# Input loaded in three parts, and the activations between two convolutions laid out with four patches interleaved, in a fused vision-tower kernel

## The reference

```
x = (x - mean) / (1e-06 + std) / sqrt(16)            # per patch and colour
x = conv2d(x, conv1_w, conv1_b); residual = x        # 3 -> 64 channels, 3x3
x = gelu(group_norm(x, gn1_g, gn1_b))                # 32 groups
x = conv2d(x, rconv1_w, rconv1_b)                    # 64 -> 64, 3x3
x = gelu(group_norm(x, gn2_g, gn2_b))
x = residual + conv2d(x, rconv2_w, rconv2_b)         # 64 -> 64, 3x3
x = conv2d(x, proj_w, proj_b, stride=16, pad=0)      # patch -> 192 numbers
```

## Time and profile before

| | |
|---|---|
| median of 3 runs | 1460.72 us (1459.5 to 1462.84) |
| profiled execution | 1465.48 us, of which the span is 1463.7 us |
| PE busy | 1365.6 us (93%) |
| DVE busy | 1081.5 us (74%) |
| ACT busy | 864.3 us (59%) |
| POOL busy | 576.4 us (39%) |
| granted TensorE clock, mean | 0.984 |

### The profile page before, as it was taken

One profiled execution on the slowest core, in us unless ns is written; L12 is line 12 of the kernel. 1 busy time (PEld: TensorE's weight loads), 2 busy tenths in 40 slices (PEclk: granted clock), 3 DMA queues, 4 the chain that ended last, 5 costly groups with the idle time before them and its releaser, 6 DMA issues.

```text
span 1463.7 us, 38493 instructions
## 1 busy us (share of the span) xinstructions
PE 1365.6 (93%) x14042; PEld 1022.2 (70%) x14042; DVE 1081.5 (74%) x4148; ACT 864.3 (59%) x2127; POOL 576.4 (39%) x1116
## 2 busy tenths in 40 slices
PE   4999988888999999999999999999999978998889
PEld 2865653344888688858976897788688867754647
DVE  3864358898888988888888889888988854544520
ACT  1434446777667777777767767767777630344451
POOL 1100035555544544544554554544545521162600
PEclk9999999999999999999999999999999988998999
DMA  7799945545554455455545554555455589300000
GB/s 218 208 268 275 266 118 162 183 127 132 139 151 134 128 150 143 131 140 143 147 125 142 150 149 119 147 152 138 128 154 136 149 226 255 79 1 1 1 1 17
DMA packets 125178, 206.17 MB, mean 141 GB/s; under 512 B 20028, under 2 KB 88188, under 8 KB 124478
## 3 DMA queue, kind: packets, MB, share of 16 engines
q1 hardware_dynamic: 124990, 203.71, 51.0%
HBM read 103.11 MB, written 20.70 MB: 85 GB/s over the span
## 4 chain that ended last, share of the span: by engine, by line
PE 63%; DMA 9%; issue 7%; DVE 7%; POOL 6%; SPq 6%; ACT 2%; POOLq 0%; ACTq 0%; DVEq 0%
PE rc L637 26%; PE pj_st L728 8%; DMA sb_acts<-sb_hst 7%; PE rc L638 6%; PE pj_st L732 4%; POOL sb_tmp L487 4%; PE rc L658 3%; PE rc L657 3%; DMA sb_wall_arena<-scratch_fold 2%; SPq L372 2%; SPq L311 2%; PE c L693 2%; DVE sb_bn L952 1%; PE rc L1440 1%; PE rc L1528 1%
## 5 line engine op out<-in xcount | busy, mean ns | idle before, releaser
L637 PE MATMUL rc<-sb_acts,sb_rwd 128*64 128x512 f16 x1764 | 559.3, 390 | 17.4 <-DMA sb_acts<-sb_hst 17.4
L638 PE MATMUL rc<-sb_acts,sb_rwd 128*64 128x512 f16 x1764 | 560.3, 390 | 0.0
L487 POOL TENSOR_TENSOR sb_tmp<-sb_mst,sb_half_neg 128x8 f32<-128x8 f32 x200 | 350.7, 1754 | 456.3 <-DVE sb_mst L973 453.4
L554 ACT ACTIVATE sb_f32q<-c,sb_gsh,sb_gsc 128x128 f32<-128x128 f32 x792 | 298.7, 458 | 273.7 <-POOL sb_gsh L497 273.7
L637 PE MATMUL rc<-sb_acts,sb_rwl 128*64 128x512 f16 x1176 | 361.8, 389 | 0.0
L638 PE MATMUL rc<-sb_acts,sb_rwl 128*64 128x512 f16 x1176 | 361.1, 389 | 0.0
L728 PE MATMUL pj_st<-sb_wall_arena 128*64 128x384 f16 x1792 | 308.6, 334 | 6.9 <-DVE sb_wall_arena L992 6.6
L576 ACT ACTIVATE sb_g2f<-rc,sb_gsh,sb_gsc 128x128 f32<-128x128 f32 x784 | 298.1, 481 | 4.5 <-POOL sb_gsh L497 4.5
L732 PEld LDWEIGHTS pj_st<-sb_wall_arena 128*64 128x64 f16 x1792 | 221.6, 221 | 62.3
L732 PE MATMUL pj_st<-sb_wall_arena 128*64 128x192 f16 x1792 | 242.8, 245 | 0.0
L728 PEld LDWEIGHTS pj_st<-sb_wall_arena 128*64 128x64 f16 x1792 | 218.8, 218 | 22.7 <-DVE sb_wall_arena L992 6.7
(11 more groups left out here) (191 smaller groups left out, 1856.3 us busy)
## 6 DMA issues: line engine op xcount, KB each, us to landing
sb_acts<-sb_hst SPq DMA_DIRECT2D x792, 78.8 KB, 2.6
sb_im<-x_planes SPq DMA_DIRECT2D x202, 136.5 KB
sb_wall_arena<-w_lo SPq DMA_DIRECT2D x48, 528.0 KB, 3.9
sb_acts<-sb_hst SPq DMA_DIRECT2D x96, 162.0 KB, 3.2
sb_wall_arena<-w_lo SPq DMA_DIRECT2D x24, 480.0 KB, 3.7
sb_f32q<-in_proj SPq DMA_DIRECT2D x12, 576.0 KB, 4.8
sb_wall_arena<-in_proj SPq DMA_DIRECT2D x12, 576.0 KB, 5.2
w_lo<-sb_wall_arena SPq DMA_DIRECT2D x8, 768.0 KB, 3.7
```

The costliest lines, as they stand in the source:

```text
L487: ch.did(gp.tensor_tensor(t1, var, half_neg[:, :], ALU.pow))
L554: ins = nc.scalar.activation(g1f[:, q * Q + m, :], c1[q][:, m * HALF:(m + 1) * HALF], ACT.Gelu, bias=gsh[q][:, m:m + 1], scale=gsc[q][:, m ...
L637: nc.tensor.matmul(out[0:CH, :], w_odd, x_odd, start=(n == 0), stop=(n == 14))
L638: yield nc.tensor.matmul(out[CH:128, :], w_even, x_even, start=(n == 0), stop=(n == 14))
```

## The change

x is loaded in three DMAs, one for each colour, and each is issued behind one of the first three doublings. DVE waits for each part before its seven `bn_stats`.

The first activations are laid out with the four patches of a slot innermost: 9 rows x 18 pixels x 4 patches. A row of a slot is 72 elements, a shift by one pixel is 4 elements, and a matmul reads 8 runs of 64 elements. `gelu1` writes with a step of four f32 values to make this layout. `split1` then reads and writes long runs. The doubling leaves out the first, zero row of the slot (72 elements in place of 18). Because the middle convolution's result has the patches innermost too, `channel_stats` of it and `gelu2_at` read PSUM with a step of four values. The first convolution's result keeps its layout.

```diff
-HB = U * PAD + WD
+HB = U * PAD + WD * Q
-        g1f = f32q[:, 0:U * HALF].rearrange("p (g n) -> p g n", g=U)
+        g1n = f32q[:, 0:U * HALF].rearrange("p (q n g) -> p q n g", q=2, g=Q)
...
-            sp.dma_start(xt, a["x"].rearrange("c p w n -> p c w n")).then_inc(s_xld, 16)
...
             for n in range(FU):
                 double_proj(n)
+                if n < C:
+                    sp.dma_start(xt[:, n], a["x"][n]).then_inc(s_xld, 16)
...
-                    sp.dma_start(acts[p][64 * half:64 * half + 64, row, q * Q * PAD + WD:(q + 1) * Q * PAD],
-                                 hst[q][64 * row:64 * row + 64, WD:Q * PAD]).then_inc(s_dup[p][q], 16)
+                    sp.dma_start(acts[p][64 * half:64 * half + 64, row, q * Q * PAD + WD * Q:(q + 1) * Q * PAD],
+                                 hst[q][64 * row:64 * row + 64, WD * Q:Q * PAD]).then_inc(s_dup[p][q], 16)
...
-                    ins = nc.scalar.activation(g1f[:, q * Q + m, :], c1[q][:, m * HALF:(m + 1) * HALF], ACT.Gelu,
+                    ins = nc.scalar.activation(g1n[:, q, :, m], c1[q][:, m * HALF:(m + 1) * HALF], ACT.Gelu,
...
-                    ins = nc.scalar.activation(g2f[:, q * Q + m, :], rc[p][q][:, m * HALF:(m + 1) * HALF], ACT.Gelu,
+                    ins = nc.scalar.activation(g2f[:, q * Q + m, :], rc[p][q][:, :].rearrange("p (n g) -> p g n", g=Q)[:, m, :], ACT.Gelu,
...
-                    return bass.AP(tensor=buf, offset=k * HB + (q * Q * SL + slot) * WD + m,
-                                   ap=[[3 * HB, 128], [PAD, Q], [WD, 8], [1, P]])
+                    return bass.AP(tensor=buf, offset=k * HB + q * Q * PAD + (slot * WD + m) * Q,
+                                   ap=[[3 * HB, 128], [WD * Q, 8], [1, P * Q]])
...
-            dve.wait_ge(s_xld, 16)
             for k in range(21):
+                if k % 7 == 0:
+                    dve.wait_ge(s_xld, 16 * (k // 7 + 1))
                 v.bn_stats(x6[:, k, :], xt[:, k // 7, k % 7, :]).then_inc(s_xch, 1)
...
-                    v.memset(t[:, 0:2, q * Q * PAD:q * Q * PAD + WD], 0.0).then_inc(s_rowz, 1)
+                    v.memset(t[:, 0:2, q * Q * PAD:q * Q * PAD + WD * Q], 0.0).then_inc(s_rowz, 1)
...
+                patch = src[:, :].rearrange("p (n g) -> p g n", g=Q) if at else src[:, :].rearrange("p (g n) -> p g n", g=Q)
                 for m in range(Q):
-                    v.bn_stats(bn6[s][:, at + m, :], src[:, m * HALF:(m + 1) * HALF]).then_inc(s_dch, 1)
+                    v.bn_stats(bn6[s][:, at + m, :], patch[:, m, :]).then_inc(s_dch, 1)
...
-                src = g1f[:, q * Q:q * Q + Q, :].rearrange("p g (r w) -> p g r w", w=P)
-                hi = hst[q][:, :].rearrange("p (g r w) -> p g r w", g=Q, r=SL)[:, :, 1:9, 1:17]
-                lo = acts[p][:, 2, q * Q * PAD:(q + 1) * Q * PAD].rearrange("p (g r w) -> p g r w", g=Q, r=SL)[:, :, 1:9, 1:17]
+                src = f32q[:, q * Q * HALF:(q + 1) * Q * HALF].rearrange("p (r n) -> p r n", r=8)
+                hi = hst[q][:, :].rearrange("p (r n) -> p r n", r=SL)[:, 1:9, Q:17 * Q]
+                lo = acts[p][:, 2, q * Q * PAD:(q + 1) * Q * PAD].rearrange("p (r n) -> p r n", r=SL)[:, 1:9, Q:17 * Q]
```

## The result

The changed kernel takes 1446.91 us, median of 4 runs (1439.52 to 1451.52), beside 1461.78 us (1459.5 to 1463.69, 4 runs) of the kernel before on the same chip. The two medians stand at 0.990; the ratio on record is 0.9878, 95% interval 0.9834 to 0.9922. The profiled execution is the shortest of the four, 1439.52 us with a span of 1437.7. One like it was forecast at 1439.5 with that span. So the forecast for the profiled pair is met to the tenth, and the medians differ by some 15 to 21 us, where 26 was forecast. Executions of one kernel spread over 4 to 21 us here.

The account below looks back on a forecast made before the run. PE was taken to bound the fold and the 144 slots with projection, DVE group 0, after a late first doubling. 8.8 + 16.8 + 0.4 = 26.0 us off the 1460.72 median gave 1434.7 us, range 1426 to 1452.

Parts of the forecast that it names:

- The start: Fold's start: with x behind the doublings PE goes on at 15.0 instead of 24.3 us; 9.3 - 0.5 = 8.8 us gained.
- a bound of 2.7: Fold's start: most that could be gained if PE's slow 1.2 GHz stretch shrank, some 13 pairs at 0.21 us each.
- 0.5 was taken: Fold's first steps: loss from doublings queued with the parts of x, bounds 0 and 3 us.
- PE's waits for doublings at 20 to 50 us: Fold: PE waiting for doublings in that stretch was named as a sign that the prediction is wrong.
- The pairs: Loop, 144 slots with projection: pairs at the fold's 0.219 us instead of 0.227 save 0.117 us a slot, 16.8 us.
- idle time in slots with projection: Loop: idle time of PE in these slots was named as a sign that the prediction is wrong.
- ACT's strided write: L554's f32 write with a 16-byte step: bounds 0 and 0.1 us a slot, 5 us in all; taken as 0.
- The smaller doubling: Slots without projection: 28 KB less a slot, 0.11 us; at most 52 x 0.11 = 5.7 us of gain.
- DVE's reads of PSUM: Four `bn_stats` of `rc` a slot with a 16-byte step: no cost taken; upper bound 0.13 us each, 0.53 a slot.
- the third rival: DVE's `bn_stats` of `rc` pay 0.13 us more each for the PSUM step, giving about 1467 us; chance 0.08.
- The first: Loop pairs don't get shorter or another chain holds the slot at 5.07; only the start gains, about 1452 us; chance 0.10.
- the second rival: Fold: the start's gain is given back as doublings queue behind the parts of x; 1443.5 us if all goes; chance 0.07.

Follow-up runs that it names:

- after_again: The changed kernel once more, with no edit, run to see how far its executions differ: 1445.91 us (6 runs), ratio 0.985 to the kernel before.
- load_only: The kernel before with only the load of x in three parts, old layout kept: 1458.13 us (12 runs), ratio 0.9934 to the kernel before.
- w1_later: The changed kernel with the small first-convolution weight copies issued in fold steps 5, 6 and 20, not 2 to 4: 1447.28 us, ratio 0.9867 to the kernel before.
- layout_only: The kernel before with only the interleaved layout, x in one load ahead of the first doubling: 1450.85 us (6 runs), ratio 0.9884 to the kernel before.
- odd_start: The changed kernel with each m = 1 pair reading one element (2 bytes) further on, so runs of 64 begin odd: 1445.86 us, ratio 0.988 to the kernel before.

## Why the prediction was right, and where not

**The start, 8.8 us forecast.** The mechanism held: PE went on at 15.06, where 15.0 was forecast. The two parts of the term were both too small and cancelled, so that the sum fits is partly luck. The gain at step 0 was 12.0 us (L535 at 20.51 against 32.52), because PE also came up to 2.4 GHz sooner; the text had that as a bound of 2.7 and took none of it. The second L535 of step 1 stood at 28.23, not at 30.6. 2.4 us of the 12.0 were given back by step 5, where 0.5 was taken and 3 was the bound. PE's waits for doublings at 20 to 50 us, which the text named as a sign of being wrong, did show: 1.19 us at step 3 and 0.23 at step 1. Left at the loop's start: 9.7.

Both profiled executions were at an end of what the others show. After the restart PE had 13 pairs at the slow pace before and none after; but after_again still had 6 and load_only 11. On the mean of the traces PE goes on 8.6 us sooner and the way from there to step 0's end is 1.2 us shorter. The four traces with x in its old place start the loop at 206.8 to 211.1 us (mean 208.9), the eight that have it in three parts, w1_later apart (204.8), at 200.0 to 203.3 (mean 201.9). That is 7.0 us, and load_only's time says 9.7 with an interval of some 6 to 13. 8.8 lies between. A part of it could be the layout's, which makes a fold step 0.06 us shorter, 1.4 us in 24; layout_only's loop starts at 211.1, so no trace shows it there.

**The pairs, 16.8 us forecast.** The slots with projection gave 17.1, and over all traces 18: 725.2 us on average in the three with the old pairs, 706.9 in the seven that have the new ones and the queue order of the loop unchanged. The size is right and the reasoning that gave it is not, in two places. The text said that the middle pair is slow because it begins 2 bytes off a word. odd_start shows that this alone costs 2 ns over the changed kernel's 0.223; it takes the 32 short runs too. And the text took 0.219 from the fold as the price of this very pattern. That row was a mixture of 0.215 and 0.222 that came from the planes' distance, which the change alters as well. The new loop happens to have nearly the same mean, (0.215 + 0.223 + 0.215) / 3 = 0.218, from another mixture. The median slot gains 0.14 us and not 0.117, which over 144 slots is 20. Some 2 us of it go into more waits for even doublings (4.9, 7.5 and 5.4 us in the three traces with the old pairs, 6.2 to 9.4 in the seven with the new), because PE reaches its seventh pair sooner (mean margin 0.84 us before, 0.58 after). That idle time in slots with projection was also a named sign of being wrong. The trace agrees with the 216 ns that the Trainium skill gives in "TensorE: Matmul & The Clock Gate", section "Back-to-back issue gap", only for runs that begin on 16 bytes; the formula has no term for the rest, and here the rest was worth the whole gain of this part.

**ACT's strided write, taken at 0.** It makes an instruction 125 ns longer but four of them only 0.13 us, since their starts stay nearly as close. The text's bound of 0.2 us for each L554 reckoned as if they ran one after the other. The median slot of group 0 went from 4.46 to 4.57 us, about as much as the four. Over 28 slots that is 3 us. That the later end of L554 is the cause is argued: no run takes its step away and changes nothing else. For it, PE's wait for L554 before the first convolution grew from 0.2 to 2.3 us in group 0. The sums over the 52 slots without projection are 239.2 to 243.7 us with the old write and 241.0 to 243.9 with the new, so the measured effect is between 0 and 3. The text took 4.40 us, DVE's own pace, for a slot of group 0 from one slot. On the mean over 24 of them it was 4.69 before, with 0.46 us of idle time on DVE, because PE also waits for the even doubling there. The smaller doubling, up to 5.7 us of gain as bounded, landed 0.1 us sooner and shows nowhere.

**DVE's reads of PSUM, taken at 0.** Right: 285 ns before and after, which closes the third rival. The reasoning was weaker than the outcome. That a step in PSUM costs ACT nothing was read from L544, a copy, beside L554, a gelu; L576, the same gelu with and without the step, settles it (478 and 481 ns). The Trainium skill's "SBUF — State Buffer", section "Door 1: The DMA port swizzle", warns that a non-contiguous pattern in PSUM slows matmuls. Taken over to the reads of other engines, as the third rival did, it isn't borne out for a step of 16 bytes: DVE takes 285 ns and ACT 478 (L576) with the step. No matmul of this kernel was tried with it.

**The first and the second rival** are out by layout_only (-17.0) and load_only (-9.7).

**The median.** 26 us were forecast, 15 and 21 were measured. The parts alone give 9.7 + 17.0, and runs of one kernel differ by more than the shortfall. Its cause stays open. 1.8 us of the profiled 26.0 were in the last slot and the tail, which the change doesn't touch but for that slot; over the traces that stage takes 286.2 to 296.3 us. What makes it vary was not tried. Two numbers of the text were off by themselves. Its bounds, 2.5 us less and 8.4 more, give 1426.3 to 1437.2 us and not 1427 to 1440. And the 0.2% that it took a measurement to tell was too little: the interval here is 0.44% either way.

## What to carry to other kernels

Look at the distance of matmul starts by position, not at a mean: the mean of 0.219 hid that the fold's pairs stood 0.215 and 0.222 apart. The moving operand was cheapest here when its runs were long and began on a multiple of 16 bytes, and dearest with many short runs on odd elements. A large load can be moved behind the first urgent transfer, but in parts: in three parts the start had 9.6 us of its gain left at step 5, in one part 2.5, because the next doubling stood behind all of it. And don't multiply an instruction's duration by its count before you have looked at the distance of their starts.

## What the runs showed of the hardware

- A pair of 512 columns starts every 0.215 us with 8 runs that begin on 16 bytes, 0.221 to 0.223 with the same runs 4 or 8 bytes off (counted from the start of the buffer), 0.2245 on odd elements, 0.218 with 32 runs on even elements, and 0.246 with 32 runs on odd ones. One rule for all five was not found.
- With a step of 16 bytes in its f32 write to SBUF an ACT instruction ends later (583 in place of 458 ns for 128 elements), but four in a row start nearly as close as before (0.35 to 0.38 us apart, before 0.34 to 0.36) and take 1.63 us in place of 1.51. A step of 16 bytes where ACT reads PSUM costs nothing (478 and 481 ns). DVE pays for a step of 512 bytes when it reads SBUF (422 to 724, 693 to 1107 ns for 512 elements) and not for 16 bytes in PSUM.
- The loop's queue lost 43 and 110 us when a load was moved by one place or one unit. The new waits of PE were 51.2 us for `im` and 93.0 us for the chunks; in the changed kernel's loop PE waited for neither.
